# Two attention layers on one Trainium2 core: every probability group of layer 1 split into two float32r parts, its values four steps behind its scores, and phi projected packed

## The reference

```python
# layer 0, xf = x as (b, c, n), 64 inner channels
g_x     = einsum('ic,bcn->bni', g_w, xf) + g_b
theta_x = einsum('ic,bcn->bni', theta_w, xf) + theta_b
phi_x   = einsum('ic,bcn->bin', phi_w, xf) + phi_b[None, :, None]
y = einsum('bnm,bmi->bni', softmax(einsum('bni,bim->bnm', theta_x, phi_x)), g_x)
x = einsum('ci,bin->bcn', W_w, y.transpose(0, 2, 1)) + W_b[None, :, None] + xf
# layer 1, 128 inner channels
q = einsum('oc,bcn->bno', Wq, xf) + bq
k = einsum('oc,bcn->bcn', Wk, xf) + bk[None, :, None]
v = einsum('oc,bcn->bno', Wv, xf) + bv
out = einsum('bnm,bmc->bnc', softmax(einsum('bnc,bcm->bnm', q, k) * c ** -0.5), v)
x = x + out.transpose(0, 2, 1)
```

## Time and profile before

| | |
|---|---|
| median of 3 runs | 3206.65 us (3205.74 to 3207.05) |
| profiled execution, its own time | 3205.62 us |
| its span | 3203.8 us |
| TensorE busy | 3167.2 us (99%) |
| GpSimd busy | 2914.2 us (91%) |
| VectorE, ScalarE busy | 2103.6 us (66%), 1865.3 us (58%) |
| mean granted TensorE clock | 0.996 |

### The profile page before, as it was taken

One profiled execution on the slowest core, in us unless ns is written; L12 is line 12 of the kernel. 1 busy time (PEld: TensorE's weight loads), 2 busy tenths in 40 slices (PEclk: granted clock), 3 DMA queues, 4 the chain that ended last, 5 costly groups with the idle time before them and its releaser, 6 DMA issues. The chain is left out here.

```text
span 3203.8 us, 42308 instructions
## 1 busy us (share of the span) xinstructions
PE 3167.2 (99%) x15684; PEld 2087.4 (65%) x15684; DVE 2103.6 (66%) x2588; ACT 1865.3 (58%) x2442; POOL 2914.2 (91%) x1546
## 2 busy tenths in 40 slices
PE   8999999999999999999999999999999999999997
PEld 4555555547777765555777776555577777777775
DVE  5555555557777765555777776555577777777773
ACT  5555555546666655554666665555466666656665
POOL 4898999988999999998899998999899999999997
PEclk9999999999999999999999999999999999999999
DMA  1000000005756640000665654000076665657575
GB/s 56 24 27 21 24 27 27 27 27 118 146 112 140 130 100 25 22 27 27 133 142 112 143 116 102 27 27 26 25 144 126 135 142 117 133 116 146 114 141 119
DMA packets 91933, 271.67 MB, mean 85 GB/s; under 512 B 10192, under 2 KB 10192, under 8 KB 91728
## 3 DMA queue, kind: packets, MB, share of 16 engines
q0 software_dynamic: 55296, 201.35, 32.5%
q1 hardware_dynamic: 36432, 67.62, 7.0%
HBM read 50.83 MB, written 16.78 MB: 21 GB/s over the span
## 5 line engine op out<-in xcount | busy, mean ns | idle before, releaser
L1134 POOL TENSOR_TENSOR p_lo<-probs,p_hi 128x1024 fp32r<-128x1024 f32 x448 | 1158.7, 2630 | 111.0 <-ACT probs L895 84.5
L390 POOL TENSOR_TENSOR sums<-sums,probs 128x1024 f32<-128x1024 f32 x448 | 1066.3, 2380 | 110.7 <-ACT probs L901 59.5
L991 DVE TENSOR_REDUCE piece_max<-rough 128x2 f32<-128x1024 f32 x504 | 616.4, 1223 | 457.1 <-PE rough L543 457.0
L901 ACT ACTIVATE probs<-scores 128x1024 f32<-128x1024 f32 x512 | 519.6, 1025 | 633.2 <-PE scores L576 624.2
L1015 DVE TENSOR_TENSOR probs<-scores,shift_rows 128x1024 f32<-128x1024 f32 x512 | 626.2, 1223 | 371.0 <-PE scores L589 364.9
L894 ACT ACTIVATE p_hi<-probs 128x1024 fp32r<-128x1024 f32 x448 | 475.0, 1060 | 550.6 <-DVE probs L1015 550.0
L985 DVE TENSOR_REDUCE piece_max<-rough 128x1 f32<-128x512 f32 x1024 | 661.1, 682 | 127.0 <-PE rough L537 127.0
L895 ACT ACTIVATE probs<-probs 128x1024 f32<-128x1024 f32 x512 | 535.6, 1046 | 89.6 <-DVE probs L1015 89.6
L585 PE MATMUL scores<-qry_a,keys_a 128*128 128x512 f32 x1024 | 446.4, 436 | 0.0
L1168 POOL DMA_DIRECT2D sent_sums<-probs x384 | 409.2, 1066 | 1.6 <-issue 1.5
L589 PE MATMUL scores<-qry_b,keys_a 128*128 128x512 f32 x1024 | 400.0, 391 | 0.0
(11 more groups left out here) (97 smaller groups left out, 4070.7 us busy)
## 6 DMA issues: line engine op xcount, KB each, us to landing
sent_sums<-probs POOLq DMA_DIRECT2D x384, 512.0 KB, 4.8
x_q<-x SPq DMA_DIRECT2D x32, 256.0 KB, 2.8
x_res<-x SPq DMA_DIRECT2D x32, 256.0 KB, 2.9
mid<-mid_new SPq DMA_DIRECT2D x32, 256.0 KB, 2.2
x_kv<-mid SPq DMA_DIRECT2D x32, 256.0 KB, 2.8
x_q<-mid SPq DMA_DIRECT2D x32, 256.0 KB, 2.7
x_res<-mid SPq DMA_DIRECT2D x32, 256.0 KB, 4.6
out<-result SPq DMA_DIRECT2D x32, 256.0 KB, 3.6
```

What stands on the lines that cost most here:

```text
L390: eng.tensor_tensor(sums[:], sums[:], probs[:, slot(st, s)], ALU.add).then_inc(s_plus, 1)
L901: nc.scalar.activation(probs[:, slot(st, s)], scores[:, s % 2], ACT.Exp, scale=SCALES[0]).then_inc(s_whole, 1)
L991: nc.vector.reduce_max(piece_max[:, t, TPG * c:TPG * (c + 1)], src, AX.X).then_inc(s_reduced, 1)
L1134: nc.gpsimd.tensor_tensor(dst, w, rd(hi), ALU.subtract).then_inc(done, 1)
```

## The change

- Layer 1: all 16 groups of a block are split. Only six groups stay whole: 12 to 15 of the first block of the last stage, which read the held values, and 5 and 10 of the very last block. `v_vals` goes, chunk 1 gets its halves like the others.
- `LAG` is 4. `p_hi` has 5 buffers in place of 4, `p_lo` has 3, and GpSimd's split of group s waits for the values of group s-3.
- The two seed adds go. SyncE copies groups 0 and 1 to the partial sums by plain DMAs (`copy_probs`), and groups 2 to 15 are sent with accumulation. The partial sums are doubled, one pair for each parity of the block; layer 0's `sums` lies in the first.
- The previous block's output is taken in step 4 (was 3) and its denominators are summed in step 6 (was 5) if it is of layer 1; reciprocal rows, normalising, finish and the projections of phi (9 to 10) and g (12 to 13) follow one step later. The steps with three rough pieces are 5, 8, 9, 12 (were 7, 8, 10, 12).
- phi is projected as two float32 matmuls with 64 weight columns and 256 data columns, to the upper and lower 64 rows of the bank, and is copied by two ScalarE instructions of 128x256 in place of four of 64x256.
- The eight moves of late values lie over three blocks (2, 4, 2), were 5 and 3 over two.
- Smaller ones: `diag` shares memory with `rdiag`, and the constant `share` is replaced by scaling the shift row by 1/64 in the copy that ScalarE makes anyway.

```diff
-HI_SLOTS = (2, 3, 0, 1)
-LAG = 3
+HI_SLOTS = (2, 3, 4, 0, 1)
+LO_BUFS = 3
+LAG = 4
-             for three in ((6, 8, 10, 12), (7, 8, 10, 12))]
+             for three in ((6, 8, 10, 12), (5, 8, 9, 12))]
-TAKE_AT = 3
+TAKE_AT = (3, 4)
-DEN_AT = 5
-RDEN_AT, RDEN_AT_PAIRS = 8, 9
+DEN_AT = (5, 6)
+RDEN_AT, RDEN_AT_PAIRS = (8, 9), 9
-FINISH_AT = (11, 9)
-PHI_AT, G_AT = (11, 9), (13, 12)
+FINISH_AT = (11, 10)
+PHI_AT, G_AT = (11, 10), (13, 13)
-MOVES_AT = ({6: 0, 8: 1, 10: 2, 12: 3, 14: 4}, {1: 5, 3: 6, 5: 7})
+MOVES_AT = {-1: {8: 0, 12: 1}, 0: {4: 2, 6: 3, 8: 4, 11: 5}, 1: {4: 6, 8: 7}}
+WHOLE_OPENING, WHOLE_ENDING = (12, 13, 14, 15), (5, 10)
-WHOLE_CHUNK = 1
-WHOLE = (2, 3)
-SEEDS = 2
-SEED_AT = {2: 0, 3: 2}
-SENT = tuple(range(4, 16))
+COPIED = (0, 1)
...
-        v_vals = sb("v_vals", [P, QB])
-        p_lo = sb("p_lo", [P, len(HI_SLOTS), GC], F32R)
+        p_lo = sb("p_lo", [P, LO_BUFS, GC], F32R)
-        sums = sb("sums", [P, GC])
-        sent_sums = sb("sent_sums", [P, TPG, GC])
+        sent_sums = sb("sent_sums", [P, 2, TPG, GC])
+        sums = sent_sums[:, 0, 0]
...
+            def copy_probs(st, s):
+                sp.wait_ge(s_whole, whole_of(st.g, s))
+                if s == COPIED[0]:
+                    sp.wait_ge(s_fold, st.g - (st.prev == 1))
+                settle(sp)
+                sp.dma_start(sent_sums[:, st.parity, s], probs[:, slot(st, s)]).then_inc(s_copied[s], 16)
...
                 load_prep(st)
                 if st.next_q:
                     load_q(st.g + 2, *st.next_q)
+                if st.layer == 1:
+                    for s in COPIED:
+                        copy_probs(st, s)
...
+            def project_halves(place, src):
+
+                for h in range(TPG):
+                    last = mm(place[half(h), 0:HALF].rearrange("p (a k) -> p a k", k=KT), wt_phi[:, half(h)],
+                              tiles_of_half(src, h), start=True, stop=True)
+                last.then_inc(p_phi, 1)
...
-                    project(free_bank, wt_phi, x_kv[:], p_phi)
+                    project_halves(free_bank, x_kv[:])
...
-                for h in range(TPG):
-                    copy(half_tiles(buf, h, 0), tiles_of_half(src, h), PHI_B[half(h)])
-                for h in range(TPG):
-                    last = copy(half_tiles(keys_a[keys], h, c), tiles_of_half(src, h), PHI_B[half(h)])
-                last.then_inc(h_phi, 1)
+                copy(buf[:, 0:HALF], src[:, 0:HALF], PHI_B)
+                copy(cols(keys_a[keys], c, HALF), src[:, 0:HALF], PHI_B).then_inc(h_phi, 1)
...
             def split_probs(st, s):
                 pool.wait_ge(s_whole, whole_of(st.g, s))
-                lo_part(p_lo[:, s % len(HI_SLOTS)], probs[:, slot(st, s)], hi_part(s), s_p_lo)
-
-            def seed(st, s):
-
-                pool.wait_ge(s_whole, whole_of(st.g, s + 1))
-                if st.prev == 1:
-                    pool.wait_ge(s_fold, st.g)
-                nc.gpsimd.tensor_tensor(sent_sums[:, s // 2], probs[:, slot(st, s)], probs[:, slot(st, s + 1)],
-                                        ALU.add).then_inc(s_seed, 1)
+                if s >= LO_BUFS:
+                    pool.wait_ge(s_used, used(st.g, s - LO_BUFS))
+                elif st.prev == 1:
+                    pool.wait_ge(s_used, used(st.g - 1, s + GROUPS - LO_BUFS))
+                lo_part(low_part(st.groups_before + s), probs[:, slot(st, s)], hi_part(st.groups_before + s), s_p_lo)
 
             def send(st, s):
 
                 pool.wait_ge(s_whole, whole_of(st.g, s))
-                if s - TPG not in SENT:
-                    pool.wait_ge(s_seed, seeded(st.nth, 2 * (s - SENT[0])))
-                else:
-                    pool.wait_ge(s_sent[s % TPG], sent(st.nth, s - TPG))
+                summed(pool, st.nth, s - TPG)
                 settle(pool)
-                nc.gpsimd.dma_start(sent_sums[:, s % TPG], probs[:, slot(st, s)],
-                                    accum_op=ALU.add).then_inc(s_sent[s % TPG], 16)
+                nc.gpsimd.dma_start(sent_sums[:, st.parity, s % TPG], probs[:, slot(st, s)],
+                                    accum_op=ALU.add).then_inc(sent_sem(st.nth, s), 16)
...
-                    if st.layer == 1 and s in HALVED:
+                    if st.layer == 1 and s not in st.whole_groups:
                         split_probs(st, s)
-                    if st.layer == 1 and s in SENT:
+                    if st.layer == 1 and s not in COPIED:
                         send(st, s)
-                    if st.layer == 1 and s in SEED_AT:
-                        seed(st, SEED_AT[s])
```

More of the change, by code:

```diff
@@ L51 @@
 V_LO_AT = 13
-WHOLE_CHUNK = 1
-WHOLE = (2, 3)
-HALVED = tuple(s for s in range(16) if s not in WHOLE)
-SEEDS = 2
-SEED_AT = {2: 0, 3: 2}
-SENT = tuple(range(4, 16))
+COPIED = (0, 1)
 class Stage:
@@ L91, in __init__ @@
         self.ends = self.nxt is None
+        self.whole_groups = WHOLE_OPENING if stage.late_values and self.opens else WHOLE_ENDING if self.ends else ()
+        self.moves = {}
+        if stage.late_values:
+            self.moves = MOVES_AT.get(i_known, {})
+        if stage.prepares == "late" and last:
+            self.moves = MOVES_AT[-1]
+        self.held_from = self.g - i_known - 1 if stage.late_values else self.g
         self.by_pair = self.nxt == 0
         self.groups_before = 2 * blocks * (i_known + (blocks if stage.late_values else 0))
+        self.prev_groups_before = 2 * blocks * (blocks - 1) if self.opens else self.groups_before - 2 * blocks
         self.next_q = None
@@ L173, in build @@
         rdiag = sb("rdiag", [P, 2, QB], F32R)
+        diag = rdiag[:, 0]
         result = sb("result", [P, QB])
@@ L362, in shifted, with fold @@
             return nth * GROUPS + s + 1
-        def fold(eng, layer, g, nth):
+        def fold(eng, layer, g, nth, parity):
             if layer == 0:
@@ L550, in shift_row @@
                 pe.wait_ge(s_done, g + 1)
-                mm(acc_out[:, parity], ones_r[:], diag[:, parity], start=True, stop=True).then_inc(s_row, 1)
+                mm(acc_out[:, parity], ones_r[:], diag, start=True, stop=True).then_inc(s_row, 1)
             def score_group(st, s, between=None):
@@ L590, in score_group, with whole_values, halved_values @@
                 last.then_inc(s_scores, 1)
-            def halved_values(b, first_block, g, nth, parity, s):
+            def whole_values(g, parity, place, s):
+                pe.wait_ge(s_whole, whole_of(g, s))
+                vals = held(s // TPG)
+                for h in range(TPG):
+                    k = slice((s % TPG * TPG + h) * KT, (s % TPG * TPG + h + 1) * KT)
+                    last = mm(acc_out[:, parity], vals[:, k], probs[:, place, h * QB:(h + 1) * QB],
+                              start=False, stop=s == GROUPS - 1 and h == TPG - 1)
+                last.then_inc(s_used, 1)
+            def halved_values(b, first_blocks, g, nth, parity, groups_before, s):
                 if s == 0:
@@ L966, in block_program @@
                         hold_v(stage.made * BLOCKS + st.i, st.i, free_bank)
[L967 to L970 removed]
+                    if s in st.moves:
+                        move_v(st.held_from, st.moves[s])
                 if st.ends:
@@ L1122, in block_program @@
                 if st.ends:
-                    fold(dve, st.layer, st.g, st.nth)
+                    fold(dve, st.layer, st.g, st.nth, st.parity)
                     reciprocals(st.g, st.parity)
@@ L1198, in block_program @@
                         split_k(stage.made * BLOCKS + st.i, stage.made_keys, st.i)
-                    if stage.prepares == "late" and st.new_keys and s - 1 in MOVES_AT[0]:
-                        c = MOVES_AT[0][s - 1]
-                        if c != WHOLE_CHUNK:
-                            split_held(stage.made * BLOCKS + c, c)
+                    if s - 1 in st.moves:
+                        c = st.moves[s - 1]
+                        split_held((stage.b if stage.late_values else stage.made) * BLOCKS + c, c)
             run_all(pool, block_program)
```

210 lines of the change are left out of this document (99 added, 111 removed).

## The result

| | before | after |
|---|---|---|
| median | 3206.19 us (3205.05 to 3207.05, 4 executions) | 3228.44 us (3228.01 to 3238.23, 4 executions) |
| span of the profiled execution | 3203.8 us | 3226.2 us |
| TensorE busy | 3167.2 us | 3161.0 us |
| GpSimd busy | 2914.2 us | 2973.5 us |

The changed kernel takes 1.0076 times as long (95% interval 1.0063 to 1.0088). I had forecast 33 us less; it is 22 us more. This is the page of the profile after: two groups of instructions with their busy time, mean length and the idle time before them, and the transfers with KB and median time to landing.

A forecast was written before the change was run, and what follows sets the result against it. TensorE, without idle time in steady blocks, was taken as the bound. Terms 23.2 + 4.9 + 3.7 + 3.0 - 4.2 + 1.5 + 1.0 = 33.1 us off 3206.65 gave 3174 us; 8-in-10 range 3164 to 3189.

The forecast's parts named there:

- GpSimd's load, layer 1: Layer 1 blocks: GpSimd's turn 2.93 us, list 50.5 to 50.9 us, 3 us to spare against TensorE; price 0.
- rival (b): GpSimd or the landings bind part of each block, 0.5 us a block, 15.5 us in all: 3189 us; chance 10%.
- Rival (c): Three `p_lo` buffers make GpSimd start group 2 too late in each block, turning the sign: 3229 us; chance 5%.
- The copies at 0: SyncE's copies of groups 0 and 1 land in 4.8 us, before send 2 asks for them; price 0.
- Late moves: First block of the last stage: four splits fewer, 9.4 us of GpSimd; gain 1.5 us (0 to 2.2).
- The last block: Very last block: GpSimd does 44.9 in place of 48.5, send chain two links longer; gain 1.0 us (-3 to 3).
- phi in L0 image 0: Layer 0, image 0: packed phi halves run side by side, saving 0.62 us for each of 8 chunks; gain 4.9 us.
- phi in layer 1: Layer 1: packed phi takes 0.63 us instead of 0.86, saving 0.23 for each of 16 chunks; gain 3.7 us.
- g one step later: L1 images 0 and 1: shift row waits 0.30 us more in each of 14 blocks; loss 4.2 us.
- the whole groups: Layer 1 values: splitting saves 0.40 us a group over 58 groups; gain 23.2 us (20.3 to 26.1).
- the opening: Opening: VectorE's chain starts 1.5 us earlier and loses 1.5 of 1.7 us of holes; gain 3.0 us (1.0 to 3.6).

The follow-up runs named there:

- e1: Changed kernel, but two of the 16 low parts of a layer 1 block made for one tile of keys instead of two: 3213.97 us, 1.0018 of before.
- e7: Changed kernel, but VectorE instead of GpSimd makes the low part of group 12, in step 14: 3222.91 us, 1.0044 of before.
- e3: Changed kernel with four buffers of `p_lo` instead of three: 3223.24 us, 1.0056 of before.
- e2: Changed kernel, but SyncE copies only 16 of the 1024 columns of groups 0 and 1: 3214.94 us, 1.0040 of before.
- e6: Changed kernel, low parts of moved values and last keys issued ahead of the step's split and send, moves as 3, 3, 2: 3222.53 us, 1.0061 of before.
- e8: Changed kernel with e6 and e7, plus VectorE making the odd groups' low parts in the last block, no group whole there: 3199.65 us, 0.9990 of before.
- e11: e8 with the full-width phi opening of e9, and VectorE making all 16 low parts of the last block: 3199.75 us, 0.9978 of before.
- e12: Kernel before with e9's phi; in the last block VectorE makes the low parts and adds groups 13 to 15, not sent: 3192.70 us, 0.9956 of before.
- e5: Kernel before with only phi packed as two column halves, opening included, copied in two pieces: 3208.96 us, 1.0005 of before, in two clusters.
- e9: Kernel before with phi packed in the stages but at full width in the opening: 3198.63 us, 0.9978 of before.

## Why the prediction was wrong, step by step

**The step that failed: "GpSimd's load, layer 1", "a turn each 2.93 us", "Price 0".** The turn is 3.23 to 3.27. I priced the send at 0.58 us, the distance from one start to the next; it takes 0.88. Fourteen sends are then 12.3 us a block, not 8.1, and two more of them than before, with waits for landings queued in the same list, put GpSimd at or over TensorE's block. It cost 19.5 us in steady blocks (e1 gives them back, e7, with all work done, all but 6.4). This is my rival (b) in kind, which I gave 10% and 15.5 us; it did not bind every block by 0.5 us, but let GpSimd begin each block a little later until it was behind, and then cost 0.7 to 3.3 us a block, or, in image 1, nothing. Rival (c), the three buffers, was the one that I had let turn the sign: e3 shows 3 to 6 us for it. That its 3229 us is nearly the time measured is chance.

**The copies at 0.** Their landing (4.0 us) was well estimated. That they cost nothing was not: e2 recovers 6.3 us in image 0. The rule of the Trainium skill that I quoted (Trainium Kernel Development and Optimization, Key Constraints: all queues share the 16 DMA engines) would allow for it, and the DMA share went from 0.64 to 0.78; that the shared engines are the way isn't shown (e2). I had used the rule only to book no gain.

**Late moves, forecast 1.5 us better, were 13.4 worse.** I counted GpSimd's work in the block, and counted it wrong: "four splits fewer" holds against a steady block of the new kernel, but the block before had 14 splits and has 12 now, two fewer (4.7 us, not 9.4), and two more sends. I also left out its order: low parts of moved values stand in line behind a step's split and send. e6 and e8 bear this out: 61.6 with another order and spread, 56.3 with GpSimd relieved too. And I had no term for the clock, some 5 of the 13.4 us; in e8 it stays at 1.00 in that block.

**The last block, forecast 1.0 better, was 6.5 worse.** GpSimd came into it late: its fold began 19.1 us after the block did (3163.1), where before it was 11.6 (3139.7). Behind it stands the chain of landings that I had bounded at 3 us. With GpSimd relieved of half its low parts there the block is 80.2 (e8), with all of them 77.4 (e11); in the kernel before, with three sends fewer as well, it goes from 75.7 to 68.4 (e12).

**Not in the prediction at all: the edges of layer 0,** 3.1 us each for images 2 and 3. Two more of TensorE's waits stand there: 0.53 for `g_vals` at the shift row, and one of 1.61 for VectorE's maxima, when normalising and `finish`, now a step later, stand in front of a reduction. These come to 2.1 us; a wait of 0.85 was there before too. That leaves about 1 us which I haven't placed. The causes are read from the trace: no kernel here tried to mend these edges.

**Right, or off in size only.**

- phi in L0 image 0: forecast 4.9, measured 4.8. The records start in pairs at the same time, and the whole takes 69.02 - 68.48 = 0.54 us, where the earlier trace rows had 1.05, and the batch before it 1.76 where it was 1.87: 0.62 a chunk, as worked out.

```profile
66.72 1.94 PE L649 MATMUL acc_out<-probs,hold 128*64 128x512 f32 x8
68.48 0.60 PE L537 MATMUL acc_out<-x_kv,const_sb 128*64 128x256 f32 x4
69.02 0.50 PE L562 MATMUL rough<-keys_a,qry_a 64*128 64x512 f32 x2
```

- phi in layer 1: forecast 3.7, measured 2.2 (e5). The matmul after phi starts 0.58 us behind it, and phi 0.32 behind the one before, 0.09 more than usual.

```profile
851.61 0.39 PE L637 MATMUL acc_out<-p_hi,v_lo 128*128 128x512 f32 x1
851.93 0.65 PE L537 MATMUL acc_out<-x_kv,const_sb 128*64 128x256 f32 x4
852.51 0.50 PE L604 MATMUL scores<-qry_a,keys_a 128*128 128x512 f32 x1
```

- g one step later: forecast 0.30 a block, measured 0.16 (the shift row starts 0.39 us after the matmul before it, not 0.53): 2.2 us, not 4.2.

```profile
925.00 0.39 PE L608 MATMUL scores<-qry_b,keys_a 128*128 128x512 f32 x1
925.39 0.50 PE L570 MATMUL acc_out<-rdiag,ones_r 128*128 128x512 f32 x1
```

- the whole groups: forecast 0.40 each; undisturbed blocks of images 2 and 3 show (55.63 - 54.99)/2 = 0.32 and (54.79 - 54.10)/2 = 0.34. With no stall anywhere, layer 1 would have gained 17.2 us with phi and g in it (4.9 + 4.8 + 5.7 in images 0 to 2 and 1.8 in the last stage's middle, from e1 and L1 image 1), where my terms for the same make 23.2 + 3.7 - 4.2 = 22.7. With layer 0 (5.0) and the opening (1.1) that is 23.3 us gained, against which 45.6 us of losses stand.
- the opening: forecast 3.0, measured 1.1. VectorE's chain runs from 15.32 to 34.5 us: it begins 0.3 earlier and loses 0.7 of its holes. In the forecast I let it begin 1.5 us earlier, by ScalarE's copies, and TensorE was as late.

## What to carry to other kernels

Where an engine's records overlap, as GpSimd's sends and its next instruction do, take its turn from the ends or from those whom it releases, over many turns, and not from two starts; here a block's list was 50.5 us by the starts and 54.7 by the ends, of 56.1. When the bound engine's list is shortened, the price of everything that another engine gets in exchange is paid in its queue order too: what waits for a landing holds all that stands behind it. And the smallest parts of a change are worth running alone: phi in the stages (e9) gives 7.6 us, and with a last block rearranged in another way 13.5 (e12), where all of the change together lost 22.

## What the runs showed of the hardware

**TensorE's clock in the opening.** With phi packed there, some executions are 11 us longer, all of it ahead of the first stage. In a profile of such a one (e7) every matmul keeps the pitch of the lower level, 1.2 GHz; in one of e8 with the same opening it halves from about 10.8 us on. Timelines of TensorE, first e7, then e8:

```profile
9.28 1.12 PE L553 MATMUL scores<-probs,const_sb 128*64 128x256 f32 x4
10.33 1.97 PE L561 MATMUL scores<-const_sb,probs 128*128 128x64 f32 x8
12.23 1.12 PE L553 MATMUL scores<-probs,const_sb 128*64 128x256 f32 x4
13.28 1.97 PE L561 MATMUL scores<-const_sb,probs 128*128 128x64 f32 x8
```
```profile
10.08 1.41 PE L561 MATMUL scores<-const_sb,probs 128*128 128x64 f32 x8
11.41 0.65 PE L553 MATMUL scores<-probs,const_sb 128*64 128x256 f32 x4
11.99 1.10 PE L561 MATMUL scores<-const_sb,probs 128*128 128x64 f32 x8
```

A chunk's two projections start 1.05 us apart in the one (12.23 to 13.28) and 0.58 in the other. The list is the same, TensorE had been fed without a gap since 7.3 and 7.1 us, and the granted clock reads 1.00 in both. In e7 the pitch stays so through all eight chunks and the pairs behind them, to about 50 us (the next queries' projection takes 1.84 us from 47.96 on), and the granted clock reads 1.00 all the while. From 35 to 40 us it reads 0.50 in e8 and in the kernel before, so the column shows some stretches at the lower level and misses this one. In the kernel before, with full-width phi, none of 26 executions was over 3209 us, and neither that nor e9 and e11 showed a second cluster. That the packed opening is the cause is shown by e5 and e9, the projection and its two copies taken together; that the level is the means is read from the pitch.

**A port between VectorE and GpSimd.** VectorE's split, with both inputs in SBUF, took 1.22 us alone (four times in e8, from 3145.6 us on, and 13 of 14 times in e12) and 3.11 and 3.40 us while a split of GpSimd ran (e8 above); VectorE's shift of the scores, which reads PSUM, stayed at 1.22. The Trainium skill (SBUF — State Buffer, SBUF: two separate sides) says that the two share a port pair as an exclusive lock when VectorE has two inputs in SBUF and GpSimd reads SBUF too; the rows agree.

**Accumulating transfers of 512 KB** had a DMA share of 0.94 at 185 GB/s when they were issued as fast as their landings allowed (e11). Whether another order of issue would have made them faster isn't shown; three transfers fewer did shorten the block (e12, together with VectorE's splits).
